# Between the scans and the experts of a one-core kernel: what is loaded, multiplied and normalised in the last scan block and beside the first expert group

## What is computed

```python
xn = (x - mu) * rsqrt(var + 1e-5) * ln_w + ln_b          # per token
xi, z = split(xn @ W_in); u = silu(conv(xi) + conv_b)
dt_r, Bm, Cm = split(u @ W_xproj); delta = softplus(dt_r @ W_dt + b_dt)
h = h * exp(delta * A) + (delta * u) * B_t               # 256 channels x 64 states, over 1024 steps
y = (h . C_t + u * D) * silu(z);  attn = x + y @ W_out
x1 = layernorm(x + attn)
for l in range(4):                                       # 4 experts, F = 512, the best 2 are used
    probs = softmax(x @ rw[l] + rb[l]);  keep the top 2, renormalised -> comb
    xhat = normalise(x)
    h = gelu((xhat * g + b) @ w1[l, e] + b1[l, e]);  y = h @ w2[l, e] + b2[l, e]
    x = sum_e comb_e * (x + y_e)
out = layernorm(x1 + x)
```

## Time and profile before

| | us |
|---|---|
| time, median of 3 runs | 2364.61 (2362.97 to 2365.02) |
| profiled execution, its own time | 2364.13 |
| its span in the trace | 2362.3 |
| DVE busy | 2026.2 (86%) |
| PE busy | 2162.7 (92%) |
| ACT busy | 1513.0 (64%) |
| POOL busy | 960.9 (41%) |

### The profile page before, as it was taken

One profiled execution on the slowest core, in us unless ns is written; L12 is line 12 of the kernel. 1 busy time (PEld: TensorE's weight loads), 2 busy tenths in 40 slices (PEclk: granted clock), 3 DMA queues, 4 the chain that ended last, 5 costly groups with the idle time before them and its releaser, 6 DMA issues. The chain is left out here.

```text
span 2362.3 us, 49990 instructions
## 1 busy us (share of the span) xinstructions
PE 2162.7 (92%) x16960; PEld 1276.8 (54%) x16960; DVE 2026.2 (86%) x2878; ACT 1513.0 (64%) x1793; POOL 960.9 (41%) x468
## 2 busy tenths in 40 slices
PE   6886999999999999999999965999999999989987
PEld 2442333333333333333333325888899989989886
DVE  4768999999999999999999956777877787787776
ACT  3767988888888888888888832343344334434332
POOL 3215344343443434434344314444444444444342
PEclk9895999999999999999999986999999999999999
DMA  4887222222212222122221240000100020000000
GB/s 135 237 244 193 44 46 41 44 42 46 45 40 44 43 45 46 40 44 43 45 46 40 45 129 27 1 0 0 37 1 0 1 72 0 0 1 6 8 5 18
DMA packets 354555, 114.91 MB, mean 49 GB/s; under 512 B 282984, under 2 KB 345072, under 8 KB 354224
## 3 DMA queue, kind: packets, MB, share of 16 engines
q1 hardware_dynamic: 349728, 110.79, 19.0%
q10 hardware_dynamic: 4752, 3.15, 0.4%
HBM read 67.98 MB, written 45.88 MB: 48 GB/s over the span
## 5 line engine op out<-in xcount | busy, mean ns | idle before, releaser
L1425 DVE TENSOR_TENSOR_SCAN arena<-behind 128x1040 f32<-128x1040 f32 x512 | 1156.9, 2309 | 7.1 <-ACT behind L923 4.5
L993 ACT ACTIVATE arena<-PS,arena 128x512 f32<-128x512 f32 x512 | 348.5, 689 | 544.2 <-PE PS L1213 543.3
L913 ACT ACTIVATE behind<-PS 128x1024 f32<-128x1024 f32 x512 | 526.6, 1029 | 133.3 <-DVE arena L1425 100.7
L1129 PE MATMUL PS<-arena 128*32 128x128 f32 x8192 | 566.0, 406 | 1.8 <-DVE arena L1425 1.8
L923 ACT ACTIVATE behind<-PS 128x1024 f32<-128x1024 f32 x512 | 539.2, 1053 | 8.0 <-PE PS L1112 3.8
L1225 PE MATMUL PS<-arena 128*128 128x128 f32 x4096 | 482.5, 277 | 24.3 <-DVE arena L1574 24.1
L1225 PEld LDWEIGHTS PS<-arena 128*128 128x128 f32 x4096 | 478.7, 194 | 36.1 <-DVE arena L1574 24.1
L716 POOL COPY behind<-carry 128x64 f32<-128x64 f32 x128 | 209.0, 1633 | 517.5 <-DVE arena L1425 377.8
L1213 PE MATMUL PS<-parts_xh,parts_w 128*128 128x512 f32 x1536 | 390.4, 408 | 26.2 <-DVE parts_w L1451 15.5
L1129 PEld LDWEIGHTS PS<-arena 128*32 128x32 f32 x8192 | 234.7, 119 | 291.4 <-issue 211.7
L1112 PE MATMUL PS<-arena 96*128 96x512 bf16 x1024 | 314.7, 389 | 54.9 <-ACT behind L923 38.7
(11 more groups left out here) (119 smaller groups left out, 1403.4 us busy)
## 6 DMA issues: line engine op xcount, KB each, us to landing
dl_d<-arena SPq DMA_DIRECT2D x48, 256.0 KB, 3.0
du_d<-arena SPq DMA_DIRECT2D x48, 256.0 KB, 3.3
arena<-dl_d SPq DMA_DIRECT2D x512, 24.0 KB
arena<-b_d SPq DMA_DIRECT2D x64, 192.0 KB
arena<-du_d SPq DMA_DIRECT2D x512, 24.0 KB
b_d<-arena SPq DMA_DIRECT2D x48, 128.0 KB, 2.7
u_d<-behind SPq DMA_DIRECT2D x8, 512.0 KB, 3.5
sz_d<-arena SPq DMA_DIRECT2D x8, 512.0 KB, 4.5
```

Of the source, the lines that this page charges most:

```text
L913: nc.scalar.activation(seg(dA[:, half])[:, :, 1:], PS[:, 0:2, :].rearrange("p j (i t) -> p (j i) t", t=TC), ACT.Exp).then_inc(exp_done, 1)
L993: nc.scalar.activation(hT[:, e % 2, c], PS[:, HIDDEN[(GT * e + c) % 3], :], ACT.Gelu, bias=bias1[:, lp, e * GT + c:e * GT + c + 1]).then_i ...
L1129: last = nc.tensor.matmul(PS[32 * j:32 * j + 32, 4 + kk, 0:DB], cd[:, pair, j, 32 * i:32 * i + 32], seg(hb[kk])[:, :, 1 + 16 * j + i], sta ...
L1425: nc.vector.tensor_tensor_scan(hb[kk][:, q * QD * SEG:(q + 1) * QD * SEG], dA[:, q % 2], dB[:, G_, lo:lo + QD * SEG], 0.0, ALU.mult, ALU.a ...
```

## The change

Only what lies between the last scans and the first expert group is written anew, with the buffers' places that it needs.

- SP: in the last block, as soon as the other block's buffers are free, `load_weights(0)`, the router's weights, b1 and the last chunk's u, silu(z) and x (into `usz_last`, `xres_last`, with a semaphore of their own). X is loaded as a first group of four tiles (`x_first`) and the other 26. The stores of x1 for the last two chunks move from ACT's queue to SP's, and layer 1's weights go behind them.
- PE: the 16 bias sums of layer 0 in four pieces in the last block; `turn` of the last chunk behind `stage_xh` of group 0, `project` of it inside the first group's products.
- ACT: w1 times g of layer 0 behind the last exponent; three `carry_state` copies that nothing reads are gone.
- POOL: no `prepare` for layer 0. `stage_scores` of group 0 stands ahead of the last chunk's rsqrt and group 1's.
- DVE: the split of w1, the bias and group 0's normalisation first; the ends of the last two chunks between the staging steps of group 0 and the normalisation of group 1.

```diff
@@ -134,8 +134,11 @@
...
-        w1_s = take(2, E, F)
+        w1_s, w2_s = [None, None], [None, None]
+        X = take(NT, H)
+        w1_s[1] = take(E, F)
+        w2_s[1] = take(E * GT, H)
+        bias1 = take(2, E * GT)
+        assert at_[0] <= HB
+        at_[0] = HB
+        w1_s[0] = take(E, F)
+        w2_s[0] = take(E * GT, H)
+        assert at_[0] == HB + RD
         w1g = take(E, F)
+        rw_s = take(NL, E, H)
+        assert at_[0] == LOWER
...
+        hT = take(2, GT, 512)
+        assert at_[0] <= BST_AT
+        at_[0] = BST_AT
+        xo = take(2, GT, H)
+        assert at_[0] <= C_IN_AT
+        at_[0] = C_IN_AT
+        b1_s = take(NL * E * GT)
+        at_[0] = USZ_AT
+        xsum_o = take(GT, H)
+        at_[0] = BST_AT
+        usz_last = take(2, HALVES, 2, TC)
+        xres_last = carry[:, 0, 0:H]
...
@@ -500,14 +543,21 @@
...
+                if last:
+
+                    sp.wait_ge(arg_ready, NQ * blk)
+                    load_weights(0)
+                    sp.wait_ge(dbp, 2 * QPG * blk)
+                    sp.dma_start(rw_s, router_w.rearrange("p (l e h) -> p l e h", l=NL, e=E)).then_inc(rw_in, 16)
+                    sp.wait_ge(c_spread, 2 * NCH)
+                    sp.dma_start(b1_s, b1).then_inc(b1_in, 16)
+                    sp.wait_ge(slot_ready, 2 * blk - 2)
+                    load_post(c, pair, usz_last, xres_last, post_last)
                 if kk == 1 and held(chunk):
...
             run_blocks(sp, emit)
-            sp.wait_ge(post_done, NCH - 1)
-            load_post(NC - 1, BP - 1)
...
             sp.wait_ge(y_done, NB - 1)
-            sp.wait_ge(carried, NB - 1)
+            sp.wait_ge(carried, CARRIED)
...
-            sp.dma_start(X[:, 0:NCH - 2], stored(0, NCH - 2)).then_inc(x_in, 16)
-            sp.dma_start(b1_s, b1).then_inc(b1_in, 16)
-            sp.dma_start(rw_s, router_w.rearrange("p (l e h) -> p l e h", l=NL, e=E)).then_inc(rw_in, 16)
...
+            sp.dma_start(X[:, 0:GT], stored(0, GT)).then_inc(x_first, 16)
+            sp.dma_start(X[:, GT:NCH - 2], stored(GT, NCH - 2)).then_inc(x_in, 16)
+            for m in range(NCH - 2, NCH):
+                sp.wait_ge(post_done, m + 1)
+                sp.dma_start(x1_d[m], x1c).then_inc(x1_out, 16)
+            load_weights(1)
             sp.wait_ge(x1_out, 16 * NCH)
             sp.dma_start(X1, stored(0, NCH)).then_inc(x_in, 16)
+            for l in range(2, NL):
+                sp.wait_ge(f_y, NG * E * (l + 1))
+                load_weights(l)
 
...
@@ -765,15 +813,11 @@
...
-            chunk_rsqrt(NCH - 2)
-            pool.wait_ge(y_done, NB - 1)
-            prepare(0, 0, 0)
-            chunk_rsqrt(NCH - 1)
...
             def begin(first_layer):
-                pool.wait_ge(f_last, 2)
-                pool.wait_ge(x_in, 16)
+                rsqrt(rs_f, f_var, f_rs, 1)
+                chunk_rsqrt(NCH - 2)
+                pool.wait_ge(arg_ready, NQ * NB)
+                pool.wait_ge(x_first, 16)
                 pool.wait_ge(rw_in, 16)
-                rsqrt(rs_f, f_var, f_rs, 1)
+                stage_scores(0, 0, 0)
+                chunk_rsqrt(NCH - 1)
                 rsqrt(rs_f, f_var, f_rs, 2)
-                stage_scores(0, 0, 0)
                 stage_exp(0)
+                pool.wait_ge(y_done, NB)
                 pool.wait_ge(b2_in, 16)
                 stage_bias(0, 0, 0)
+                pool.wait_ge(x_in, 16)
...
@@ -957,10 +1005,15 @@
...
-                    if q == Q_CARRY and held(blk):
+                    if q == Q_CARRY and held(blk) and not (isinstance(c, int) and c == NC - 1 and pair + kk):
                         carry_state(*((c, pair, 0) if kk else (c, 0, 1) if pair else (c - 1, 1, 1)))
...
+                if last:
+                    act.wait_ge(f_w[0], F_LOADS)
+                    for e in range(E):
+                        nc.scalar.activation(w1g[:, e], w1_s[0][:, e], ACT.Identity, scale=g_s[:, e:e + 1]
+                                             ).then_inc(f_g, 1)
...
@@ -972,13 +1025,8 @@
...
             evacuate(NC - 1, BP - 1, 0)
-            store_x1(NCH - 2)
             evacuate(NC - 1, BP - 1, 1)
-
-            act.wait_ge(carried, NB - 1)
             act.dma_start(b2_s, b2.rearrange("p (l e h) -> p l e h", l=NL, e=E)).then_inc(b2_in, 16)
-            store_x1(NCH - 1)
...
+            def bias_of_first(e):
+
+                if e == 0:
+                    pe.wait_ge(f_w[0], F_LOADS)
+                    pe.wait_ge(evac_done, 2 * QPG * NB)
+                for c in range(GT):
+                    ec = e * GT + c
+                    last = nc.tensor.matmul(PS[:, 3, ec:ec + 1], w1_s[0][:, e, c * P:(c + 1) * P],
+                                            lb_s[:, e:e + 1], start=True, stop=True)
+                if e == E - 1:
+                    last.then_inc(f_bp, 1)
 
...
-                if part == Q_PROJECT:
+                if part == 1:
                     project(NCH - 2)
-            turn(NCH - 1)
-            project(NCH - 1)
...
-                bias_of_offset(*first_layer)
+                pe.wait_ge(evacuated, NB - 1)
                 stage_xh(0, 0)
+                pe.wait_ge(p_link, (NCH - 2) * P_LINKS + 1)
+                turn(NCH - 1)
+                pe.wait_ge(f_bias, 1)
                 pe.wait_ge(f_xhTs, 1)
...
+                if isinstance(n, int) and n == 0:
+                    project(NCH - 1)
...
             dve.wait_ge(scan_done, NB * NQ)
-            for m in range(NCH - 2, NCH):
-                if m == NCH - 1:
-                    split_w1(0, 0)
-                    gate(m)
-                add_residual(m)
-                chunk_stats(m)
-                chunk_aggregate(m)
-                chunk_norm(m)
+            dve.wait_ge(arg_ready, NQ * NB)
+            nc.vector.memset(order, 0.0).then_inc(f_sum, FS0)
+            dve.wait_ge(f_sum, FS0)
+
+            def keep(m):
+
                 dve.wait_ge(y_done, NB - 1)
                 dve.wait_ge(post_done, m + 1)
                 nc.vector.tensor_copy(X[:, m], x1c).then_inc(f_last, 1)
-            dve.wait_ge(carried, NB - 1)
-
-
-            dve.wait_ge(post_done, NCH)
-            dve.wait_ge(f_w[0], F_LOADS)
-            nc.vector.memset(order, 0.0).then_inc(f_sum, FS0)
-            dve.wait_ge(f_sum, FS0)
-
-            dve.wait_ge(x_in, 16)
-            dve.wait_ge(f_last, 2)
...
-                add_bias(0, 0)
-                stage_norm(0, 0, 0)
-                stage_norm(1, 1, 1)
+                upper_w1(0, 0)
+                dve.wait_ge(y_done, NB - 1)
+                add_bias(0, 0, True)
+                dve.wait_ge(x_first, 16)
+                stage_moments(0, 0)
+                lower_w1(0, 0)
+                stage_scale(0, 0, 0)
+                add_residual(NCH - 2)
+                chunk_stats(NCH - 2)
+                chunk_aggregate(NCH - 2)
                 split_xh(0, 0)
+                gate(NCH - 1)
+                chunk_norm(NCH - 2)
+                keep(NCH - 2)
                 stage_scores(0, 0)
+                add_residual(NCH - 1)
+                chunk_stats(NCH - 1)
+                chunk_aggregate(NCH - 1)
+                dve.wait_ge(x_in, 16)
+                stage_moments(1, 1)
+                stage_scale(1, 1, 1)
                 stage_router(0, 0)
+                chunk_norm(NCH - 1)
+                keep(NCH - 1)
                 sum_bias(0)
```

More of the change, by code:

```diff
@@ L328, in build @@
         post_in = sem("post_in")
+        post_last = sem("post_last")
+        x_first = sem("x_first")
         post_t = sem("post_t")
@@ L438, in run_blocks, with usz_of, xres_of, await_post @@
                 emit(NC - 1, b // NBLK, b % NBLK, b == BP * NBLK - 1)
+        def usz_of(m):
+            return usz_last if isinstance(m, int) and m == NCH - 1 else usz
+        def xres_of(m):
+            return xres_last if isinstance(m, int) and m == NCH - 1 else xres
+        def await_post(eng, m):
+            if isinstance(m, int) and m == NCH - 1:
+                eng.wait_ge(post_last, 80)
+            else:
+                eng.wait_ge(post_in, 80 * m + 80)
+        def turned(m, h):
+            return PS[:, 7, P + h * P:2 * P + h * P] if isinstance(m, int) and m == NCH - 1 else PS[:, 6, h * P:(h + 1) * P]
+        def projected(m):
+            return PS[:, 7, 3 * P:] if isinstance(m, int) and m == NCH - 1 else PS[:, 7, 0:P]
+        def xh_bank(n):
+            return 4 if isinstance(n, int) and n == 0 else 5
         def held(count):
@@ L501, in load_c, with load_post @@
                 sp.dma_start(c_in_s, c_d[it].rearrange("b n t -> (b n) t")[:, bass.ds(t, TC)]).then_inc(c_in, 16)
-            def load_post(c, pair):
+            def load_post(c, pair, usz, xres, landed):
                 it, t = pair * 2 + c // CPT, c % CPT * TC
@@ L508, in load_post, with load_weights @@
                         sp.dma_start(usz[:, i, h, :, :], dram[it, :, h * P:(h + 1) * P, bass.ds(t, TC)]
```

(14 more changed lines are left out.)

85 lines of the change are left out of this document (41 added, 44 removed).

## The result

| | us |
|---|---|
| time, median of 4 runs | 2322.31 (2321.28 to 2322.38) |
| before, median of 4 runs | 2364.61 |
| ratio, 95% interval | 0.9823 (0.9809 to 0.9837) |
| span of the profiled execution | 2319.5 (before 2362.3) |

The account below looks back on a forecast made before the run. It took the 83.1 us from the last scan's end to the first `add_expert` as the bound. New terms summed to 45.2, saving 37.9 to 40.2; 38.5 was taken, so 2364.61 becomes 2326 us, range 2320 to 2334.

Parts of the forecast that it names:

- What bounds the stretch, and that the rest runs on unchanged: From the last scan's end to the first `add_expert`, 83.1 us, is all the change can affect; later groups keep 26.6 us.
- In the last block: Weights arrive in time, multiplication hidden, last sums 1.2 us later, and no scan moves.
- PE and DVE to the first product: After the last scan: X's tiles +3.9, DVE's tokens +9.2, PE free +9.6, first product +11.7 us against +60.2.
- the 11.4 us rival: Opening late: X's first tiles landing after 11.4 us lengthen the stretch by up to 7.5, giving 2334; 12 in 100.
- First product is not the kernel's saving; the queues of DVE and POOL are: First product's 48 us is not all gained: DVE's queue lengthens, and POOL's exponent behind two rsqrts costs about 3.8.
- The three terms of exclusion: DVE stands still beside POOL in norm and copy (0.7, twice) and group 1's scale (up to 0.9); together 0 to 2.3.
- the third case: Group 1's scale on DVE held up beside POOL's exponent, a rest of up to 0.9 us.
- TensorE's clock: Two PE waits of 5 to 10 us in the first group lower its clock; 3 us lost, 2329; 7 in 100.
- The slower case: PE stays at 1.2 GHz over whole expert groups, up to doubling their 26.6 us; three give 2406; 3 in 100.

Follow-up runs that it names:

- u1: Changed kernel with layer 0's weights, b1 and router weights loaded behind X again, and the multiplication and bias sums behind the last sums; 2347.83 us.
- u2: Changed kernel with both last chunks' ends ahead of group 0's normalisation again, all loads still early; 2332.53 us.
- u3: Changed kernel with all 16 bias sums in one piece on PE behind the last chunk's `turn`, not in the last block; 2325.36 us.
- u5: Changed kernel with X's two loads asked for in the other order, the 26 tiles ahead of group 0's four; 2329.63 us.
- u6: Changed kernel with group 0's exponent ahead of both rsqrts on POOL and the router ahead of group 1's scale on DVE; 2320.45 us.
- u8: Changed kernel with group 1's moments and scale earlier, exponent ahead of the last chunk's rsqrt, and POOL's scores waiting for scale and `start_sum` every group; 2285.46 us.
- a0_again: The changed kernel measured once more without any edit; 2322.34 us.
- u4_pool_mul: Changed kernel with w1 times g moved from ACT back to POOL, still with early weights, beside the last block's scans; 2328.56 us.

## Why the prediction was right, and where it was off

- *What bounds the stretch, and that the rest runs on unchanged*: right. u1 and u2 show the two halves, late weights (25.6 with what an idle PE adds) and chunk ends in series (9.5). The rest stayed at 892. The two halves are not a sum: the edits act on one path, and no run undoes both.
- *In the last block*: right. Weights in time, multiplication hidden (1381.72 to 1384.27 on ACT), the scans at their 2.24 us, PE's last sums over at +9.2 where it was +8.4, 0.8 later (1.2 forecast). The forecast that the scans end within a microsecond of 1387 was too narrow for the scatter of the opening part (1385.2 here). Not foreseen was that the bias pieces also hold X's first load back: without them DVE's moments started 1.3 us sooner (u3).
- *PE and DVE to the first product*: +11.5 for +11.7 (the terms as listed, 9.6 + 0.6 + 1.3, give 11.5 too). X's tiles at +3.1 for +3.9. That this load has no cover behind it, as the 11.4 us rival said (7.5 lost), u5 confirmed with 6.4 for tiles 6.5 late.
- *First product is not the kernel's saving; the queues of DVE and POOL are*: right. It came 48.7 us sooner and the kernel gained 42. The exponent waited 3.7 for a forecast of 3.8, and u6 gave 2.5 of it back.
- *The three terms of exclusion*: the step that was mis-sized. I booked 0.7 + 0.9 + 0.7 and measured 0.35 + 0 + 0. DVE did stand still in the norm (3.19 for 0.35, beside the scores) and in the copy (3.45 for 0.23, beside the bias product), but each ended within 0.1 us of POOL's operation, for whose result DVE had to wait anyway. And group 1's scale took 1.14 although three of its four instructions started while the exponent ran, so the third case did not exist. Without these terms and with the 0.35 (the copy of 0.23 behind the norm) the sum is 43.25; the missing 1.1 come from the scores' end, +14.7 for +16.0, less 0.3 in the small steps behind it. Of this 1.3, 0.8 is X's earlier arrival; PE has no part in it: what the scores need of PE, `project(NCH-2)`, was done at 1388.03 + 0.71, 4.6 us before DVE used it.
- *From the stretch to the median*: 40.9 in the stretch, 42.3, 41.9 and 41.1 in the medians on three chips. The difference to the forecast of 38.5 is thus 2.4 us of sum (1.35 from the three terms, as 0.6 of their 1.95 had been taken off already, and 1.1 from the earlier scores) and up to 1.4 of scatter.
- *TensorE's clock*: of the two waits of 5 to 10 us forecast for PE in the first group only one came. For group 1's tokens it waited 0.39, for the first `add_expert` 11.0, and the 64 products behind that took 9.52, where 64 in u8's later groups took 7.31. Their clock:

```profile
1428.60:1433.00 4.40, 4.36 (x20) 4.39 (x21) 4.26 (x8) 0.00 (x0) 0.29 (x1) 0.50 0.02 5
```

The next group still came after 26.65: the slack covered it, as booked. The slower case did not come.

The Trainium skill ("SBUF — State Buffer", section "Who interferes with whom") says that a copy or a tensor_scalar can contend with GpSimd, and that a DVE instruction with two SBUF inputs contends with a GpSimd instruction that reads SBUF. Beside POOL's wide products the trace agrees (3.45, 3.19 and 5.37 us). Beside the exponent it does not: the four L1548 took 1.14 together, the first started 0.06 us ahead of L826, the other three inside its 3.06. The measurement decides; why the exponent leaves DVE alone no run here shows.

## What to carry to other kernels

Between two phases look for the load that waits for a buffer of the old phase, and move the new phase's buffers onto what is free one block earlier; then look at the order in which the engines' queues hold the rest, since undoing the early loads gave back 25.6 of 40.9 us and undoing the order alone 9.5. A stall beside another engine's operation is nearly free if its result is what you wait for next (0.35 and 0 us here). If not, it costs up to its whole length (4.0 of 4.2 us in u8's stretch), or what is left until another engine sets the pace (0.95 of 4.2 in u8's groups, where that was PE): check which before you book it. In a loop body even the smaller price adds up: one wait in POOL's step gave 33.6 us, four fifths of what the whole change gave.

## What was not expected of the hardware

- PE's granted clock fell to 0.69 and 0.53 right behind 3.5 us in which it was busy without a pause, with products of one column (u3_bias_behind); the same 16 sums in four pieces among the last block's work left it at 1.00 (a0_again). What made it fall there no run shows by itself.
- With scans 2.7 us apart instead of 2.24 PE was busy for 3.94 of 6 us, and its clock went to 0.76 and then to 0.50 in the scan block (u4_pool_mul).
- The 16-element power on POOL (2.9 to 3.1 us) does not hold DVE up; products of 2048 elements (3.6 to 4.6 us) held a copy, a tensor_scalar and instructions with two SBUF inputs until they ended.
